# Relative attention rewritten: fp32 scores in 32x32 tiles, one merged bias band per query tile, row sums by a ones column, the triangle mask on GpSimd

## The reference

```python
x = x + rel_attention(layernorm(x), ...)   # the stage that changes
x = x + moe(layernorm(x), ...)
x = x + window_attention(layernorm(x), ...)
x = x + moe(layernorm(x), ...)
```

```python
rp = clip(j - i, -31, 31) + 31                          # bucket of query i, key j
attn = einsum('bhid,bhjd->bhij', q, k)                  # q = scaled
attn += take_along_axis(einsum('bhid,hdm->bhim', q, rpe_k_table), rp)
attn += swapaxes(take_along_axis(einsum('bhjd,hdm->bhjm', k * scale, rpe_q_table), rp))
attn = softmax(attn)
out = einsum('bhij,bhjd->bhid', attn, v)
S = segment_sum(attn, rp)                               # probabilities summed by bucket
out += einsum('inbh,hnd->bhid', S, rpe_v_table)
return out_in_token_order @ w_proj.T + b_proj
```

## Time and profile before

| what | us |
|---|---|
| median of 3 runs | 4701.89 (4697.29 to 4708.14) |
| the profiled execution's own time | 4712.8 |
| its span | 4711.0 |

### The profile page before, as it was taken

How to read it: one execution, slowest core, us unless ns; L and a number is a source line. 1 busy time by engine, 2 the same in 40 slices (tenths; PEclk the granted TensorE clock), 3 DMA queues, 4 the chain that set the end, 5 groups by cost and what they waited for, 6 DMA issues and landing times. The chain is left out here.

```text
span 4711.0 us, 85627 instructions
## 1 busy us (share of the span) xinstructions
PE 3972.3 (84%) x27720; PEld 3159.9 (67%) x27720; DVE 2794.0 (59%) x6190; ACT 1958.2 (42%) x4694; POOL 1120.2 (24%) x969
## 2 busy tenths in 40 slices
PE   4888888888888759579999389888899869489998
PEld 3656565665566558468888267777777768478887
DVE  3667666666666546865555445545455456855554
ACT  1555455555555313034444144444444423044443
POOL 1344334343434100023333100000000000033432
PEclk9999899999999879789999599999999969699999
DMA  4556455464656351034433400000000042054442
GB/s 178 177 193 211 159 179 195 166 204 157 204 174 205 124 189 69 18 130 119 127 111 81 142 12 11 15 13 14 14 13 14 10 151 81 4 165 111 127 118 49
DMA packets 348863, 522.09 MB, mean 111 GB/s; under 512 B 106192, under 2 KB 256592, under 8 KB 334928
## 3 DMA queue, kind: packets, MB, share of 16 engines
q1 hardware_dynamic: 188752, 416.74, 24.8%
q10 hardware_dynamic: 135168, 67.13, 5.0%
q0 software_dynamic: 24576, 33.57, 4.2%
HBM read 303.44 MB, written 213.91 MB: 110 GB/s over the span
## 5 line engine op out<-in xcount | busy, mean ns | idle before, releaser
L2040 POOL TENSOR_TENSOR a_win<-a_win,a_tri 128x512 f32<-128x512 f32 x256 | 326.4, 1288 | 226.0 <-DMA a_win<-band 218.2
L1993 ACT ACTIVATE a_prob<-a_ps_s,a_low 128x512 f32<-128x512 f32 x512 | 349.3, 693 | 12.7 <-DVE a_low L2136 12.7
L2136 DVE TENSOR_REDUCE a_low<-a_ps_s 128x2 f32<-128x1024 f32 x256 | 313.4, 1224 | 8.8
L1915 PE MATMUL a_ps_p<-a_ident,a_prob 128*128 128x128 f32 x2048 | 305.8, 284 | 0.6 <-ACT a_probT L2011 0.3
L2034 POOL TENSOR_TENSOR a_tri<-a_lower,a_edge 128x512 f32<-128x512 f32 x128 | 133.4, 1042 | 710.1 <-ACT a_edge L1962 696.1
L1915 PEld LDWEIGHTS a_ps_p<-a_ident,a_prob 128*128 128x128 f32 x2048 | 245.4, 147 | 67.0 <-issue 51.0
L2146 DVE CUSTOM_DVE_ANT_0 a_junk<-a_prob,a_lower 128x128 f32<-128x128 f32 x512 | 255.2, 525 | 17.2 <-DVE a_o L2107 17.2
L1907 PE MATMUL a_ps_s<-a_ident,a_win 128*128 128x128 f32 x1024 | 261.6, 339 | 0.0
L2142 DVE COPY a_probT<-a_ps_p 128x512 f32<-128x512 f32 x256 | 174.8, 683 | 138.7 <-PE a_ps_p L1915 138.6
L1492 POOL TENSOR_TENSOR b_rrms<-b_ms,b_minus_half 128x2 f32<-128x2 f32 x32 | 22.6, 707 | 961.1 <-DVE b_ms L1522 961.1
L1476 ACT ACTIVATE b_prob<-b_score,b_low 128x256 f32<-128x256 f32 (+1 forms) x512 | 240.6, 473 | 24.7 <-PE b_ps_p L1418 23.8
(11 more groups left out here) (381 smaller groups left out, 11696.3 us busy)
## 6 DMA issues: line engine op xcount, KB each, us to landing
band<-a_band SPq DMA_DIRECT2D x256, 384.0 KB, 4.6
a_win<-band SPq DMA_DIRECT2D x256, 384.0 KB, 5.3
prob<-a_prob ACTq DMA_DIRECT2D x128, 384.0 KB, 3.7
xnT<-n_xnT SPq DMA_DIRECT2D x32, 512.0 KB, 3.0
a_bins<-prob ACTq DMA_DIRECT2D x128, 128.0 KB, 3.7
fe_gT<-in_WgT SPq DMA_DIRECT2D x16, 1024.0 KB, 4.9
fe_uT<-in_WuT SPq DMA_DIRECT2D x16, 1024.0 KB, 5.3
fe_dT<-in_WdT SPq DMA_DIRECT2D x16, 1024.0 KB, 5.0
```

The costliest lines, as they stand in the source:

```text
L1915: mm = nc.tensor.transpose(ps_p[k % 2][:, c * P:(c + 1) * P], prob[:, t % 2, h, 32 + c * P:32 + (c + 1) * P], ident[:, :])
L1993: nc.scalar.activation(prob[:, t % 2, h, 32:32 + T], ps_s[k % 2][:, r, :], ACT.Exp, bias=low[:, k % 2, r:r + 1], accum_out=rsum[:, p, t, h ...
L2040: nc.gpsimd.tensor_tensor(square, square, tri[:, d, :, :], ALU.add).then_inc(win_ready, 1)
L2136: nc.vector.reduce_max(low[:, k % 2, :], both[:, :, :], AX.X, negate=True).then_inc(maxed, 1)
```

## The change

The stage `relative_stage` and its orders are rewritten; the other stages stay as they are.

- Scores are fp32 matmuls of 32x32 places: the four heads are the four groups of 32 rows, strips of 32 queries the four groups of 32 columns; each strip has one matmul for the keys before it (`k_low`) and one for the rest (`k_up`). Two extra rows of q and k carry the end buckets. All four banks of a tile are filled in one step `scores` t (0 to 3). The split, the stacks, the triangles, and the key windows' matmuls are gone.
- Query and key bias are merged into one band for a query tile. `g_pos`, `g_low`, `g_up` are the key's part with keys in columns; it goes through DRAM with a shift (`shift` scratch, `gbias` to `shifted`, ten DMAs a unit), is added to the query's part (`s_neg`, `s_pos`), and turned by `band` 0 and 1 (eight transposes). GpSimd corrects it (`sums`). Then come four stores of 63 columns and four window loads a unit, in place of eight and eight.
- Row sums come out of `values` by a column of ones in v. What is below the diagonal is no longer summed by VectorE: GpSimd masks the turned probabilities (`mask`, one operation a tile), and TensorE adds them times `v_step` in a step `lower`.
- All four kinds of turned things share the two banks `ps_p`; steps run ahead by different numbers of units (`LEAD`): q and v three, k and the g steps two, s and band one. Turning and values of a tile are one and two tiles behind its scores. q, k and v are kept for all four groups.
- VectorE has a written order of its own. The accumulator reads of the exponentials go.

```diff
+LEAD = {"q": 3, "v": 3, "k": 2, "g_pos": 2, "g_low": 2, "g_up": 2, "s_neg": 1, "s_pos": 1, "band": 1, "bins_T": -1, "bins": -1, "out": -1}
+RELATIVE_PROLOGUE = [
+    ("q", 0, 0), ("k", 0, 0), ("g_pos", 0, 0), ("g_low", 0, 0), ("g_up", 0, 0), ("v", 0, 0),
+    ("q", 1, 0), ("k", 1, 0), ("s_neg", 0, 0), ("s_pos", 0, 0), ("band", 0, 0), ("band", 0, 1),
+    ("g_pos", 1, 0), ("g_low", 1, 0), ("g_up", 1, 0), ("q", 2, 0), ("v", 1, 0), ("v", 2, 0),
+]
 RELATIVE_ORDER = [
+    ("scores", 0), ("k", 0), ("probs_T", 0), ("probs_T", 1), ("values", 0), ("s_neg", 0), ("probs_T", 2), ("lower", 0), ("probs_T", 3),
+    ("scores", 1), ("g_pos", 0), ("probs_T", 4), ("probs_T", 5), ("values", 1), ("s_pos", 0), ("probs_T", 6), ("lower", 1), ("probs_T", 7),
+    ("scores", 2), ("g_low", 0), ("probs_T", 8), ("probs_T", 9), ("values", 2), ("g_up", 0), ("band", 0), ("probs_T", 10), ("lower", 2), ("probs_T", 11), ("band", 1),
+    ("scores", 3), ("q", 0), ("bins_T", 0), ("probs_T", 12), ("probs_T", 13), ("bins_T", 1), ("values", 3), ("v", 0), ("probs_T", 14), ("bins", 0), ("lower", 3), ("probs_T", 15), ("out", 0),
 ]
+RELATIVE_SCALAR_ORDER = [
+    ("k", 0), ("probs_T", 0), ("probs_T", 1), ("home", 0), ("exp", 0), ("probs_T", 2), ("exp", 1),
+    ("g_pos", 0), ("probs_T", 4), ("home", 1), ("exp", 2), ("probs_T", 6), ("exp", 3),
+    ("g_low", 0), ("probs_T", 8), ("home", 2), ("exp", 4), ("band", 0), ("exp", 5), ("band", 1),
+    ("q", 0), ("bins_T", 0), ("probs_T", 12), ("home", 3), ("exp", 6), ("bins_T", 1), ("probs_T", 14), ("exp", 7),
+]
+RELATIVE_VECTOR_ORDER = [
+    ("max", 0), ("max", 1), ("s_neg", 0), ("probs_T", 3), ("o", 0),
+    ("max", 2), ("max", 3), ("probs_T", 5), ("s_pos", 0), ("probs_T", 7),
+    ("max", 4), ("max", 5), ("probs_T", 9), ("g_up", 0), ("probs_T", 10), ("probs_T", 11),
+    ("max", 6), ("max", 7), ("probs_T", 13), ("v", 0), ("bins", 0), ("probs_T", 15), ("out", 0),
+]
...
 # SyncE
+            def windows(b, g):
+                u = NG * b + g
+                for j in range(2):
+                    if not (isinstance(u, int) and u < 2):
+                        hold(sp, maxed, 2 * NT * (u - 1), held)
+                    hold(sp, band_ready, 2 * u + j + 1, held)
+                    for t in (2 * j, 2 * j + 1):
+                        sp.dma_start(scratch["band"][g % 2, t].rearrange("p (h x) -> p h x", h=HG)[:, :, 0:XB - 1], band[:, t, :, 0:XB - 1]).then_inc(band_out[j], 16)
+                for t in range(NT):
+                    hold(sp, band_out[t // 2], 32 * u + 32, held)
+                    rows_at = scratch["band"][g % 2, t]
+                    skewed = bass.AP(rows_at.tensor, rows_at.offset, [[W4 - 1, P], [1, W4]])
+                    sp.dma_start(win[:, g % 2, t, :, :].rearrange("p h x -> p (h x)"), skewed).then_inc(win_in[t], 16)
...
+            def unit(b, g):
+                if has_step(b, g, "band", 0):
+                    windows(*unit_after(b, g, 1))
+                if g == 1 and not (isinstance(b, int) and b == B - 1):
+                    hold(sp, emptied, section(b, NG - 1, "k") + 1, held)
+                    load_x(b + 1)
+                if has_step(b, g, "k", 0):
+                    key_bias(*unit_after(b, g, 2))
+                if has_step(b, g, "out", 0):
+                    store(*unit_before(b, g, 1))
...
 # TensorE
                 if kind in ("q", "k"):
                     if kind == "q" and g == 0:
                         pe.wait_ge(xT_in, 16 * b + 16)
...
+            def scores(b, g, t):
+                n = tile_number(b, g, t)
+                hold(pe, emptied, section(b, g, "k") + 1, held)
+                if not (isinstance(n, int) and n == 0):
+                    hold(pe, exped, HG * n, held)
+                for up in range(2):
+                    for i in range(4):
+                        own = t * P + 32 * i
+                        keys, cols = ((k_low, slice(0, own)), (k_up, slice(own, T)))[up]
+                        if own == 0 and not up:
+                            continue
+                        for h in range(HG):
+                            r = slice(32 * h, 32 * h + 32)
+                            last = nc.tensor.matmul(ps_s[h // 2][32 * i:32 * i + 32, h % 2, cols], q[r, g, own:own + 32], keys[r, g, cols], start=True, stop=True)
+                last.then_inc(scored, 1)
...
+            def lower(b, g, t):
+                pe.wait_ge(masked, tile_number(b, g, t) + 1)
+                for h in range(HG):
+                    last = nc.tensor.matmul(ps_o[32 * h:32 * h + 32, t * P:(t + 1) * P], v_step[:, g, h, :], below[:, t % 2, h, :],
+                                            start=False, stop=True, skip_group_check=True)
+                last.then_inc(lowered, 1)
...
+                    elif kind == "values":
+                        values(*tile_before(b, g, k, 2))
+                    elif kind == "lower":
+                        lower(*tile_before(b, g, k, 2))
...
 # VectorE
+            def take(b, g):
+                dve.wait_ge(lowered, NT * (NG * b + g) + NT)
+                nc.vector.tensor_copy(oT[:, :], ps_o[:, :]).then_inc(o_taken, 1)
...
+                    elif kind == "o":
+                        take(*unit_before(b, g, 1))
```

More of the change, by code:

```diff
@@ L1598 @@
-RELATIVE_SCALAR_ORDER = scores_later(RELATIVE_ORDER, (1, 1, 3, 6, 5, 5, 5, 2))
-A_NEXT = ("q", "k", "v", "q_band", "k_band", "q_stack", "k_stack")
-A_PAST = ("bins_T", "bins", "out")
+LEAD = {"q": 3, "v": 3, "k": 2, "g_pos": 2, "g_low": 2, "g_up": 2, "s_neg": 1, "s_pos": 1, "band": 1, "bins_T": -1, "bins": -1, "out": -1}
+TURNED = ("probs_T", "band", "bins_T", "out")
+WHOLE = ("q", "v", "k", "g_pos", "g_low", "g_up", "s_neg", "s_pos", "bins")
+TABLES = ("g_pos", "g_low", "g_up", "s_neg", "s_pos")
@@ new lines, in relative_steps, with number_in, count @@
+def relative_steps(b, g, order):
+    return [step for step in order if has_step(b, g, *step)]
+PAST_STEPS = [("probs_T", h) for h in range(HG)] + [("values", 0), ("lower", 0), ("values", 1), ("lower", 1), ("bins_T", 0), ("bins_T", 1), ("bins", 0), ("out", 0)]
+def number_in(kinds, b, g, kind, k):
+    def count(b, g):
+        return sum(step[0] in kinds for step in relative_steps(b, g, RELATIVE_ORDER))
+    early = sum(step[0] in kinds for step in RELATIVE_PROLOGUE)
+    if kind == "probs_T":
+        home = unit_moved(b, g, 1) if k >= (NT - 1) * HG else (b, g)
+        k = (k + HG) % (NT * HG)
+    else:
+        home = unit_moved(b, g, -LEAD[kind])
+    b, g = home
+    if isinstance(b, int):
+        u = NG * b + g
+        if u < 0:
+            return (0, [step for step in RELATIVE_PROLOGUE if step[0] in kinds].index((kind, u + LEAD[kind], k)))
+        before = early + sum(count(n // NG, n % NG) for n in range(min(u, NG * B)))
+        steps = relative_steps(b, g, RELATIVE_ORDER) if u < NG * B else PAST_STEPS
+        return (0, before + [step for step in steps if step[0] in kinds].index((kind, k)))
+    each = count(1, 0)
+    before = early + count(0, 0) + each * (g - 1)
+    return (each * NG, before + [step for step in RELATIVE_ORDER if step[0] in kinds].index((kind, k))), b
@@ new lines, in values @@
+            def values(b, g, t):
+                wait_copied(pe, b, g, "probs_T", range(HG * t, HG * t + HG))
+                if t == 0 and not (isinstance(b, int) and NG * b + g == 0):
+                    pe.wait_ge(o_taken, NG * b + g)
+                for c in range(NT):
+                    for h in range(HG):
+                        last = nc.tensor.matmul(ps_o[32 * h:32 * h + 32, t * P:(t + 1) * P], v[:, g, 0 if c < t else 1, c, h, :],
+                                                probT[:, t % 2, h, c * P:(c + 1) * P], start=(c == 0), stop=False, skip_group_check=True)
+                last.then_inc(valued, 1)
@@ L2042, in unit, with sums @@
[L2042 to L2047 removed]
+            def sums(b, g, ch):
+                for j in range(2):
+                    pool.wait_ge(copied[bank_of(b, g, "band", j)], earlier_in_bank(b, g, "band", j) + 1)
+                    n = 2 * (NG * b + g) + j
+                    if not (isinstance(n, int) and n == 0):
+                        pool.wait_ge(band_ready, n)
+                    half = band[:, 2 * j:2 * j + 2, :, :]
+                    ch.link(nc.gpsimd.tensor_tensor(same[:, :, :, :].rearrange("p t h x -> p (t h) x"), query_same[:, :].unsqueeze(1).to_broadcast([P, 2 * HG, 32]),
+                                                    half[:, :, :, XB - 1:].rearrange("p t h x -> p (t h) x").to_broadcast([P, 2 * HG, 32]), ALU.mult))
+                    near = half[:, :, :, 0:32].rearrange("p t h x -> p (t h) x")
+                    nc.gpsimd.tensor_tensor(near, near, same[:, :, :, :].rearrange("p t h x -> p (t h) x"), ALU.add).then_inc(band_ready, 1)
@@ new lines, in _ @@
+            for kind, u, k in RELATIVE_PROLOGUE:
+                if kind in ("v", "g_up", "s_neg", "s_pos"):
+                    empty(kind, 0, u, ch)
+            units(nc.vector, unit)
```

(6 more changed lines are left out.)

721 lines of the change are left out of this document (373 added, 348 removed).

## The result

The changed kernel takes 4793.88 us (median of 4 runs, 4788.89 to 4808.4) against 4699.59 for the kernel before beside it (4 runs, 4694.7 to 4708.14): ratio 1.0204, 95% interval 1.0177 to 1.0231, so **slower, by 94 us**; the interval lies wholly above 1, but does not tell whether it is more or less than 2%. Forecast were 4777 and a range of 4640 to 4900. The direction, the size and the largest single wait were right. Inside the sum the clock was charged far too much and two waits were missing, and these errors nearly cancelled.

The account below looks back on a forecast made before the run. TensorE was taken as the bound, though not saturated, with waits paid again as half-speed work. Quarters -93, a_xT wait +87, clock +67 and edges +14 sum to +75: 4788 profiled, 4777 as median; range 4640 to 4900.

Parts of the forecast that it names:

- Quarters at full clock: Relative stage, a unit from scores to scores: four longest chains sum to 41.6 us against 44.5, -93 us over 32 units.
- Quarter 0: First quarter of a unit: scores, k, then ScalarE's written order, 10.1 us; TensorE's own work 7.1, so it waits 3.0.
- quarter 1: Second quarter: VectorE's copy of ps_o waits for `lower` ahead of the maxima; 11.6 us, TensorE idle for nearly 5.
- quarter 3: Fourth quarter of a unit: TensorE's own row of work plus 1.5 us of waits for copies and banks, 12.1 us.
- S = 1.4: New score step, sixteen array places of 512 key columns in fp32: 1.4 us taken, near the lower end of its bounds.
- The rival of strict order: Score step: matmuls start strictly in program order, so 1.9 us a step, +64 us, 4840; chance 0.13.
- The wait for a_xT: Once per sequence, q's projection waits for x, loaded behind the windows' round trip: 12 to 12.5 us, seven times, +87 us.
- The clock: TensorE's granted clock halved after waits: 4.5 us a unit, 2.1 more than before, +67 us.
- Edges: Before first scores 60 us instead of 35.7; last three units skip work, about -12; net +14 us (0 to 40).
- x arrives in time: Rival: SyncE gets through its round trip early, so x's load causes no wait: -87, 4690, about no change; chance 0.07.
- both score rivals: Score step: strict order 1.9 us, 4840, chance 0.13; or head rows don't overlap, 3.6 us, 5059, chance 0.06.
- The clock holds: Rival: clock loss as before (0 instead of 67) and score step 1.0 us: about 4659; chance 0.27.

Follow-up runs that it names:

- the copy late: Changed kernel with VectorE's copy of ps_o moved behind the sum of s_pos, instead of ahead of the third maximum: 4597.12 us, ratio 0.9771.
- doubling: Kernel with a_xT early and ps_o copied late (4484 us), every tile's group of score products issued twice: 4642.21 us, ratio 0.9867.
- the last experiment: Changed kernel with GpSimd's two band sums ahead of the triangle mask in the third quarter: 4720.77 us, ratio 1.0041.
- the filler: Kernel with s_pos behind lower(1) (4743.45 us), that product issued five times instead of once: 4701.68 us, ratio 0.9985.

## Why the prediction was right, and which steps were not

- **Quarters at full clock, 41.6.** Where no other wait comes in they are 8.86, 12.16, 7.83 (this one read with the copy late) and 12.36: 41.2. Quarter 0 was put 1.2 too long and quarter 1 0.6 too short; the terms of quarter 3 add up to 12.1 only with 0.9 for both `bins_T` together. The chain in quarter 1, VectorE's copy of ps_o ahead of the maxima, is shown by its removal.
- **S = 1.4** was right: 1.32 in the trace, 1.24 by doubling. The rival of strict order came from a rule of the Trainium skill ("TensorE: Matmul & The Clock Gate", Part 3, Packing small matmuls). The trace does not agree with the use that I made of it: sixteen fp32 products of 384 to 480 columns lie within 1.10 us. The same section of the Trainium skill gives a measured speedup of 10.6 for a pack of sixteen 32x32 tiles. The trace comes near it: 16 x 0.9 us in series, an estimate from half a projection, against the measured 1.32 is 10.9.
- **The wait for a_xT, +87.** Right in place and count (7), short in size: 15.9 us each instead of 12.4, and 117 us when it was removed. 2.7 us of it are the mask ahead of the sums on GpSimd, by the last experiment. The working said that the masks "end before `lower` asks for them", which is so, and did not ask who stands behind them. The landing of a_xT took 6.7 us and not 4.5, so some other term of the 12.4 was put too long.
- **The clock, +67: wrong.** I charged 4.5 us a unit, and the loss is about 2: the unit from 1248.00 to 1291.23 takes 43.2 at a clock of 0.92 where the quarters' 41.2 stand against it, and all of the difference is in its third quarter (9.85 instead of 7.83). Over all 32 units the third quarters are 51 us longer than 7.83, 1.6 a unit. That is no more than the 2.4 before, so the term is near zero or just below it. The 5 us wait costs about 2 us in the quarter behind it (9.7 against 7.8, shown by the filler and by the late copy), where up to 3.5 was allowed; quarter 1 itself, for which a doubling of its first 5.9 us was feared, is 12.16 with the wait in it. The long wait costs 1.7 us beside itself: its quarter is 30.0 us against 12.36, and 15.9 of the 17.6 more is the wait. And quarter 0 waits 1.3 us, not 3, at a clock of 1.00. The granted clock of the stage, 0.87, was as forecast (0.83 to 0.9), but that mean is no measure of the loss: the lowest clock (0.71 in the quarter with the long wait) stands beside a wait, where little work is there to be slowed.
- **Not in the working at all:** s_neg's sum waiting for a_shifted, at the end of SyncE's queue. It lengthens quarter 1 from 12.16 to 13.3 and 14.1 in second and fourth units. The prediction followed the windows and a_xT through that queue and stopped one transfer short. The interleaved round trips gave 58 us for it, from a kernel that had a_xT early and more of this wait (150.4 us), and the sums ahead of the mask 73 for it and a part of a_xT's wait.
- **Nor the loop:** 54 us in the changed kernel, five jumps back and 0.4 us in each unit inside. How much of it the kernel before pays was not tried; its own waits of that kind in the stage are less than half:
```profile
PE a_ps_s L1900 <- issue: 17.6, 5, 3.8
```
They bear on a reading of the prediction all the same. Its slower four units, 872.60 to 1066.00, end with one of these gaps (3.5 us), and its four at full clock, 1306.20 to 1484.10, have none. So the 2.4 us a unit that it laid to the clock hold such gaps too: 17.6 us over 32 units are 0.55 of it.
- **Edges, +14:** 52.0 us from first projection to first scores instead of 35.7, where 60 was estimated: +16. What the end skips was put at -12; by the sum below, first and last units gave some -9 together.

The sum, from the trace of the changed kernel, each part as what it adds to 32 units of 41.21 us: the quarters with the long wait +123.7 (7 x 17.7), the third quarters behind their wait +50.9, the second quarters over 12.16 (a_shifted for the most part) +44.6, the fourth and first quarters at the five jumps +53.3, what the first and last units skip and the rest -9.4. Then (41.21 - 44.5) x 32 = -105.3 for the quarters, and -75.6 for what the kernel before lost against its own 44.5. Together that is +82.2, the measured lengthening of the stage; with +16 ahead of the first scores it is +98, and the medians differ by 94. Against the forecast: the clock had 144 us of losses (4.5 x 32) where the third quarters show 51, 93 too many, and a_shifted and the jumps, 98 together, were missing. The forecast was right because the direction and the largest single wait were found; that it came within 17 us is luck.

Of the signs that the prediction named, the wait of q's matmul for xT, the clock and the score groups of 1.3 us came as said. Units did not: the second of a batch takes 61 to 63 us, some 18 more than the third and not 12, and the fourth, with the jump and a_shifted, 50 to 53. VectorE's wait for ps_o was 5.7 us and not 8.

The rivals: "x arrives in time" and both score rivals are refuted. "The clock holds" was half true: the granted clock fell, to 0.87 from 0.95, but its cost stayed what it had been, and other waits stood in its place. S = 1.0, its other half, was not so.

## What to carry over

Count a queue to its last entry. When a transfer, a sum or a mask is given to a lightly loaded engine, write down what stands behind it and who waits for that; here the order on an engine busy 16% of the time cost 73 us, and SyncE's 175 (117 for a_xT and 58 for the round trips). Here two round trips through memory shared one queue, and first legs ahead of second legs beat one whole trip after the other by 58 us. And a change that lowers every engine's busy time but leaves one step at the wrong place in a written order is only half made: the same work went from 4794 to 4391 us by three reorderings and a loop written out.

## What the runs showed of the hardware

- A program can get faster by giving TensorE more work: 3.4 us of repeated products in a wait of 5 us took 42 us off it, with the granted clock of the stage at 0.93 instead of 0.88.
- Each of five jumps back of a loop cost some 9 us on balance, as waits that no releaser explains, with a body of four units (some 2100 matmul records); and first and last quarters of the units inside the loop took 0.4 us more together than outside it or with the loop written out.
- The window stage, whose code no kernel here changed, took 1170.0 us in the profiled execution before and 1151.0 in the one after (1145.8 to 1170.0 over all traces), at clocks of 0.94 and 0.95. Why was not tried. A single execution's span is therefore no measure of an edit worth 10 or 20 us in another stage.
```profile
2670.20:3840.20 1170.00, 1010.96 (x6336) 820.86 (x6336) 582.26 (x1910) 491.94 (x1561) 101.67 (x106) 0.94 0.09 29
```
```profile
2771.30:3922.30 1151.00, 999.79 (x6336) 811.99 (x6336) 583.96 (x1910) 492.55 (x1561) 101.93 (x106) 0.95 0.09 29
```
